# A two-layer graph kernel on one core: first-layer products two slots behind instead of three, the per-turn chain and the held-back products at other slots

## The chip, the cores and the metric

One core of one Trainium2 chip runs the whole kernel. The time is the device time of one execution in microseconds (us). The engines are TensorE (PE, matmuls; PEld is its weight load), VectorE (DVE), ScalarE (ACT), GpSimd (POOL) and SyncE (SP, which here only issues transfers). Sixteen DMA engines move data between memory and the on-chip buffers.

## The reference, cut to what matters

```python
def _L0_gnn_ref(z, dist, W, B):                    # N = 4096, D = 128
    msg = z @ W + B
    sens = exp(-(1.0 / dist - 1.0) ** 2 / 0.5)
    return where(dist < 1.0, sens, 0.0) @ msg      # 4096x4096 @ 4096x128

def _L1_gnn_ref(x, adj, W):
    A_hat = adj + eye(4096)
    d = sum(A_hat, axis=1) ** -0.5
    return relu((d[:, None] * A_hat * d[None, :]) @ (x @ W.T))

h = maximum(layernorm(x), 0);  x = x + _L0_gnn_ref(h, adj, L0_W, L0_B)
h = maximum(layernorm(x), 0);  x = x + _L1_gnn_ref(h, adj, L1_W)
```

Both layers multiply by the same 64 MB matrix `adj`, all in float32. The second layer's product for a block of columns needs `support`, the scaled rows of the second layer's input, and those exist only when the first layer has finished the same rows.

## The kernel before, in words

`adj` is cut into 8 by 8 blocks of 512 by 512. The row block is the **turn** g (0 to 7), and the eight column blocks of a turn are visited in the order `ORDER[g]`; each block is a **unit** u = 8g + idx, 0 to 63. Every engine has a hand-written program that loops over the units; what an engine does in its pass u is here called its **slot** u. Engines are tied only by semaphores, so one can be some slots ahead of another, but each keeps its own order.

For unit u: SP loads a pair of units (2 MB in 16 transfers, L282) into one of 3 `raw` buffers. DVE transposes the block into one of 4 `kept` buffers (L651) and writes the masked copy into one of 5 `wt` buffers (`cut`, L666). ACT does the logarithm (L531), the inversion (L536), a square (L541) and the final exponential (L547 or L550), in the order log(u), square(u-1), invert(u), weigh(u-1); in turns 0 to 2 the square of an odd unit is done by DVE instead (`quad`, L672). PE then multiplies: `multiply_weights` (L380) for the unit LAG = 3 slots back, eight matmul instructions into the accumulator `acc0`. A `wt` buffer is free again for `cut(u)` when the products of unit u-5 are done.

The second layer uses the same transposed block. If its column block lies below the turn, `mix_once` (L393) multiplies it at once from `kept`. Otherwise SP writes it to memory (`store`, L293, 1 MB) and it comes back through POOL's queue (L348) for a **late job** `mix_late` (L402), at the slots of the table `JOBS`, the rest in `TAIL`. DVE's transposition of unit u+4 waits until the 1 MB write of unit u has landed. In turns 0 to 2 PE also sums the block's rows (`sum_tiles`, L410); later DVE does that (L659).

Between turns there is a **chain** for the finished row block g-1, spread over slots of turn g: ACT copies the row sums (`copy_sums`, L558, idx 1) and PE turns them (`turn_sums`, L417, idx 2); ACT copies the accumulator (`copy_x1t`, L576, idx 2, after the last product of turn g-1, and before weigh(u-1) on ACT); PE transposes it (L433, idx 3); DVE reads the sums (`own_rows`, L734 or L739, idx 3) and makes the new rows and their normalisation (`make_x1`, L748 to L766, idx 4); ACT takes `log_pows` (L580) and copies (`copy_hid`, L588, idx 4) what PE transposed (`turn_hid`, L439, idx 5); PE multiplies (L445, idx 6); DVE writes `support` (L777, idx 7). In turns 6 and 7 ACT also empties a second-layer bank (`evict`, L592, in its slots 48 and 56), and PE's `mix_once` of those slots waits for it.

The masks for the row sums (`make_quads`, L723 and L726, 20 small DVE instructions) are made in DVE's slot 2. At the head DVE has only `take_moments(0)` (from L687) before the first `adj` pair lands.

The order within PE's slot before the change, which the change rearranges:

```python
if 1 <= g <= PE_SUMS and idx == 2: turn_sums(g - 1)
if g < PE_SUMS: sum_tiles(u)
if at_once(u) and idx < G - 1 and not (g >= 6 and idx == 0): mix_once(u)
if g >= 1 and idx == 3: turn_x1(g - 1)
if g >= 1 and idx == 5: turn_hid(g - 1)
if u >= LAG: multiply_weights(u - LAG)
if g >= 1 and idx == 6: multiply_support(g - 1)
# then the late jobs of u, then mix_once of the last idx
```

Of the kernel before, what the change touches and what calls it, by code (L numbers as in the profile page):

```python
# [18 lines left out]
G = 8  # L19
# [2 lines left out]
B = 32  # L22
T = 4
RAW, KEPT, WTS, LATE = 3, 4, 5, 3
LAG = 3
PAIRS = G * C4
UNITS = 2 * PAIRS

# [27 lines left out]
def once_count(u):  # L56
# [2 lines left out]

JOBS = {17: [(0, 0)], 25: [(0, 1)], 28: [(1, 1)],
# [4 lines left out]
TAIL = [(2, 6), (3, 6), (4, 6), (5, 6), (6, 6), (0, 5), (0, 6), (1, 6),  # L67
        (2, 7), (3, 7), (4, 7), (5, 7), (6, 7), (7, 7), (0, 7), (1, 7)]
IN_TURN = [job for u in sorted(JOBS) for job in JOBS[u]]
# [5 lines left out]
PE_SUMS = 3  # L75


def squared_by_dve(u):

    return u < PE_SUMS * G and u % 2 == 1  # L80


def dve_squares(u):
# [25 lines left out]
def slot_count(j):  # L109

    return sum(late_slot(i) == late_slot(j) for i in range(j + 1))


def build(nc, x, adj, w0, b0, w1, out):
# [6 lines left out]
    with ctx:  # L121
# [230 lines left out]
        def _(pe):  # L352
# [44 lines left out]
            def mix_late(j, bank, start, stop):  # L397
                r, c = LOADED[j]
                slot = late_slot(j)
                pe.wait_ge(late_loaded[slot], 16 * slot_count(j))  # L400
                for k in range(T):
                    mm = nc.tensor.matmul(bank[:], support[:, c * T + k, :], late_tile(slot)[:, k, :],  # L402
                                          start=(start and k == 0), stop=(stop and k == T - 1))
                mm.then_inc(late_done, 1)
# [9 lines left out]
            def turn_sums(g):  # L414
                pe.wait_ge(sums_copied, g + 1)
                for a in range(T):
                    mm = nc.tensor.matmul(side[:, a:a + 1], hid_t[:, a * P:(a + 1) * P], thirty_second[:],  # L417
                                          start=True, stop=True)
                mm.then_inc(quads_summed, 1)

            def sum_quads(g):
                pe.wait_ge(summed, C4 * (g + 1 - PE_SUMS))
                if g == PE_SUMS:
                    pe.wait_ge(quads_done, 2)
                nc.tensor.matmul(side[:, 0:T * Q * C4], quad_sum[:].rearrange("p q i -> p (q i)"),
                                 rowpart[:, g % 2].rearrange("p a q c -> p (a q c)"),
                                 start=True, stop=True).then_inc(quads_summed, 1)
# [8 lines left out]
            def turn_hid(g):  # L436
                pe.wait_ge(hid_done, g + 1)
                for a in range(T):
                    last = nc.tensor.transpose(side[:, a * P:(a + 1) * P], hid[:, a, :], ident[:])  # L439
                last.then_inc(hid_turned, 1)  # L440

            def multiply_support(g):
                pe.wait_ge(hid_t_done, g + 1)
                for a in range(T):
                    mm = nc.tensor.matmul(side[:, a * P:(a + 1) * P], hid_t[:, a * P:(a + 1) * P], w1t[:],  # L445
                                          start=True, stop=True)
                mm.then_inc(sup_multiplied, 1)
# [8 lines left out]
            for u in range(UNITS):  # L456
                g, idx = u // G, u % G
                if g == 0 and idx % 2 == 0:
                    turn_h0(idx // 2)
                    multiply_msg(idx // 2)  # L460
                if 1 <= g <= PE_SUMS and idx == 2:
                    turn_sums(g - 1)
                if g > PE_SUMS and idx == 1:
                    sum_quads(g - 1)
                if g < PE_SUMS:
                    sum_tiles(u)
                if at_once(u) and idx < G - 1 and not (g >= 6 and idx == 0):
                    mix_once(u)
                if g >= 1 and idx == 3:
                    turn_x1(g - 1)  # L470
                if g >= 1 and idx == 5:
                    turn_hid(g - 1)
                if u >= LAG:
                    multiply_weights(u - LAG)
                if g >= 1 and idx == 6:
                    multiply_support(g - 1)
                for i, (r, c) in enumerate(JOBS.get(u, [])):
                    mix_late(first_job(u) + i, mix[r], r == 0 and c == 0, (r, c) in ((0, 4), (1, 5)))
                if g >= 6 and idx == 0:
                    mix_once(u)  # L480
                if g >= 1 and idx == G - 1:
                    mix_once(u)
# [14 lines left out]
            for t, (r, c) in enumerate(TAIL):  # L497
                if t == 0:
                    sum_quads(G - 1)
                if t < LAG:  # L500
                    multiply_weights(UNITS - LAG + t)
                if t == 4:
                    turn_x1(G - 1)
                if t == 5:
                    turn_hid(G - 1)
                if t == 6:
                    multiply_support(G - 1)
                if (r, c) == (1, 6):
                    pe.wait_ge(sup_done, G)
                if c == G - 1 and r == 2:  # L510
                    pe.wait_ge(sup_done, G)
                if (r, c) == (G - 1, G - 1):
                    for k in range(T):
                        mm = nc.tensor.matmul(tail_bank[r][:], support[:, c * T + k, :],
                                              kept[:, (UNITS - 2) % KEPT, k, :], start=False, stop=(k == T - 1))
                    mm.then_inc(late_done, 1)
                else:
                    mix_late(loads, tail_bank[r], (r, c) in ((0, 5), (1, 6)), c == G - 1)
                    loads += 1
                if c == G - 1:  # L520
                    ended += 1
                    if ended >= 2:
                        turn_out(ended - 2)
# [3 lines left out]
        def _(act):  # L527
# [50 lines left out]
            def log_pows(g):  # L578
                act.wait_ge(pows_done, g + 1)
                nc.scalar.activation(inv[:], pows[:], ACT.Ln).then_inc(pows_ln, 1)  # L580
# [5 lines left out]
            def copy_hid(g):  # L586
                act.wait_ge(hid_turned, g + 1)
                nc.scalar.copy(hid_t[:], side[:]).then_inc(hid_t_done, 1)  # L588
# [11 lines left out]
            for u in range(UNITS):  # L600
                g, idx = u // G, u % G
                log(u)
                if u >= 1 and not squared_by_dve(u - 1):
                    square(u - 1)
                if g >= 1 and idx == 4:
                    log_pows(g - 1)
                invert(u)
                if g >= 1 and idx == 2:
                    copy_x1t(g - 1)
                if u >= 1:  # L610
                    weigh(u - 1)
                if g == 0 and idx in (1, 3, 5):
                    std_rows((idx + 1) // 2)
                    copy_h0((idx + 1) // 2)
                if 1 <= g <= PE_SUMS and idx == 1:
                    copy_sums(g - 1)
                if g >= 6 and idx == 0:
                    evict(g - 6)
                if g >= 1 and idx == 4:
                    exp_pows(g - 1)  # L620
                    copy_hid(g - 1)
            square(UNITS - 1)
            weigh(UNITS - 1)
            copy_x1t(G - 1)
# [13 lines left out]
        def _(dve):  # L638
# [140 lines left out]
                last.then_inc(sup_done, 1)  # L779

            take_moments(0)
            for u in range(UNITS):
                g, idx = u // G, u % G
                turn(u)
                if g < PE_SUMS:
                    cut(u)
                    if u >= 1 and squared_by_dve(u - 1):
                        quad(u - 1)
                elif u >= 1 and squared_by_dve(u - 1):
                    quad(u - 1)  # L790
                if idx % 2 == 1 and g >= PE_SUMS:
                    row_sum(u // 2)
                if g == 0 and idx % 2 == 0:
                    invert_std(idx // 2)
                    if idx < 6:
                        take_moments(idx // 2 + 1)
                    if idx == 2:
                        make_quads()
                elif g == 0:
                    make_msg(idx // 2)  # L800
                if g >= 1 and idx == 3:
                    own_rows(g - 1)
                if g >= PE_SUMS:
                    cut(u)
                if g >= 1 and idx == 4:
                    make_x1(g - 1)
                if g >= 1 and idx == 7:
                    make_support(g - 1)
            own_rows(G - 1)
            make_x1(G - 1)  # L810
# [54 lines left out]
```

## Time and profile before

| | |
|---|---|
| median of 3 runs | 616.36 us (614.26, 616.36, 616.45) |
| profiled execution | 612.92 us, of which span 611.1 us |
| mean granted TensorE clock | 0.958 of full |
| PE busy | 530.7 us, 87% |
| DVE busy | 484.6 us, 79% |
| ACT busy | 465.2 us, 76% |
| moved by DMA | 145.19 MB, 238 GB/s on average |

The span runs from the first to the last instruction; the execution has 1.8 us more around it. "Busy" is the sum over an engine's instructions; a "granted clock" of 1.00 is 2.4 GHz and of 0.5 is 1.2 GHz. The DMA share is the mean busy share of the 16 DMA engines, and can come out a little above 1.

### The profile page before, as it was taken

To read this page: it belongs to the slowest core of one execution; us is meant where nothing else is said; L and a number is where in the kernel's file an instruction comes from. 1 tells how busy PE (TensorE), PEld (TensorE's weight loads), DVE (VectorE), ACT (ScalarE), POOL (GpSimd) and SP (SyncE) were. 2 spreads that over 40 slices of the span, in tenths; PEclk is the share of its full clock that TensorE was granted. 3 is DMA by queue.
4 is the path that set the end of the run, shared out by engine and by line. 5 is a ranking of instruction groups with operands and counts; after the bars stand their busy time and mean duration, and the time that the engine had idled before them with its cause. 6 is when DMAs were issued, how large, how long until landed. Compare 5 with 4: busy or idle time off the path is not lost.

```text
span 611.1 us, 4804 instructions
## 1 busy us (share of the span) xinstructions
PE 530.7 (87%) x1509; PEld 241.9 (40%) x1509; DVE 484.6 (79%) x555; ACT 465.2 (76%) x306; POOL 39.6 (6%) x68
## 2 busy tenths in 40 slices
PE   2446897789869999688999999799999999999994
PEld 1233443233324444333444444344444444445442
DVE  2899998689978899999999989965999589102156
ACT  2387898799889879999999899984999497910010
POOL 0340500000000000000000000000000000201000
PEclk9997997979998999899899999989999999999998
DMA  7999999999999589979997799896798410497122
GB/s 172 222 257 313 322 303 323 325 312 285 338 319 308 130 241 312 309 175 316 320 234 206 207 297 309 240 224 188 232 238 242 113 52 21 163 423 305 69 66 73
DMA packets 93340, 145.19 MB, mean 238 GB/s; under 512 B 10369, under 2 KB 84354, under 8 KB 84354
## 3 DMA queue, kind: packets, MB, share of 16 engines
q1 hardware_dynamic: 88274, 108.17, 65.9%
q0 software_dynamic: 5040, 36.70, 16.3%
q8 instruction: 12, 0.20, 0.1%
q14 instruction: 14, 0.11, 0.1%
HBM read 106.04 MB, written 38.80 MB: 237 GB/s over the span
## 4 chain that ended last, share of the span: by engine, by line
PE 50%; ACT 25%; DVE 18%; issue 4%; SPq 2%; DMA 1%; DVEq 0%
PE acc L380 18%; PE mix L393 12%; PE mix L402 12%; ACT wt L531 6%; ACT wt L541 6%; DVE kept L651 6%; ACT wt L550 5%; ACT wt L536 5%; DVE wt L666 4%; DVE wt L672 2%; PE acc L402 2%; PE mix L410 1%; DVE msg L713 1%; PE side L402 1%; SPq L282 1%
## 5 line engine op out<-in xcount | busy, mean ns | idle before, releaser
L380 PE MATMUL acc<-wt,msg 128*128 128x512 f32 x512 | 239.5, 612 | 4.7 <-ACT wt L550 4.7
L666 DVE SCALAR_TENSOR_TENSOR wt<-kept 128x2048 f32<-128x2048 f32 x64 | 146.5, 2289 | 21.1 <-PE acc L380 19.7
L651 DVE STREAM_TRANSPOSE kept<-raw 128x2048 f32<-128x2048 f32 x64 | 147.5, 2304 | 7.3 <-DMA raw<-in_adj_dram 5.7
L380 PEld LDWEIGHTS acc<-wt,msg 128*128 128x128 f32 x512 | 97.5, 197 | 130.4 <-issue 123.9
L531 ACT ACTIVATE wt<-wt 128x2048 f32<-128x2048 f32 x64 | 121.9, 1905 | 25.4 <-DVE wt L666 25.4
L536 ACT ACTIVATE wt<-wt 128x2048 f32<-128x2048 f32 x64 | 121.7, 1901 | 0.3
L393 PE MATMUL mix<-kept,support 128*128 128x512 f32 x224 | 103.7, 609 | 7.8 <-ACT mixed L592 4.7
L550 ACT ACTIVATE wt<-wt 128x2048 f32<-128x2048 f32 x52 | 98.8, 1901 | 0.0
L541 ACT ACTIVATE wt<-wt 128x2048 f32<-128x2048 f32 x52 | 98.8, 1900 | 0.0
L402 PE MATMUL mix<-late,support 128*128 128x512 f32 x208 | 93.5, 592 | 0.0
L659 DVE TENSOR_REDUCE rowpart<-raw 128x16 f32<-128x4096 f32 x20 | 87.6, 4378 | 0.0
L393 PEld LDWEIGHTS mix<-kept,support 128*128 128x128 f32 x224 | 42.9, 195 | 62.8 <-issue 54.3
L402 PEld LDWEIGHTS mix<-late,support 128*128 128x128 f32 x208 | 39.3, 190 | 48.3 <-issue 48.3
L410 PE MATMUL mix<-kept,ones 128*32 128x512 f32 x192 | 31.1, 726 | 23.9 <-DVE kept L651 23.9
L348 POOL DMA_DIRECT2D late<-adj_t_spill x26 | 13.9, 535 | 468.4 <-PE mix L402 391.5
L672 DVE SCALAR_TENSOR_TENSOR wt<-wt 128x2048 f32<-128x2048 f32 x12 | 27.5, 2289 | 17.3 <-ACT wt L536 17.3
L576 ACT COPY x1t<-acc 128x512 f32<-128x512 f32 x8 | 4.6, 580 | 41.5 <-PE acc L380 41.5
L748 DVE TENSOR_TENSOR x<-side,x 128x512 f32<-128x512 f32 x8 | 5.5, 688 | 28.6 <-PE side L433 28.6
L635 ACT COPY kept<-mix 128x512 f32<-128x512 f32 x6 | 3.5, 585 | 29.9 <-PE mix L402 26.6
L333 POOL TENSOR_SCALAR support<-x,mv 128x128 f32<-128x128 f32 x24 | 20.1, 856 | 47.1 <-DVE mv L691 47.1
L547 ACT ACTIVATE wt<-wt 128x2048 f32<-128x2048 f32 x12 | 22.8, 1898 | 0.0
L819 DVE TENSOR_TENSOR kept<-mix,support 128x512 f32<-128x512 f32 x6 | 4.1, 690 | 19.2 <-PE mix L491 19.2
(87 smaller groups left out, 256.7 us busy)
## 6 DMA issues: line engine op xcount, KB each, us to landing
raw<-in_adj_dram SPq DMA_DIRECT2D x512, 128.0 KB, 5.7
adj_t_spill<-kept SPq DMA_DIRECT2D x35, 1024.0 KB, 10.2
late<-adj_t_spill POOLq DMA_DIRECT2D x26, 1024.0 KB, 7.9
raw<-adj_t_spill POOLq DMA_DIRECT2D x9, 1024.0 KB, 9.1
x<-in_x_dram SPq DMA_DIRECT2D x32, 64.0 KB, 2.8
out_dram<-kept SPq DMA_DIRECT2D x32, 64.0 KB, 1.8
w_sb<-in_L_gnn_W_dram SPq DMA_DIRECT2D x1, 64.0 KB
late<-in_L_gnn_W_dram SPq DMA_DIRECT2D x1, 64.0 KB
```

The source lines that it names most:

```text
L380: mm = nc.tensor.matmul(acc0[:], msg[:, col(u) * T + k, :], wt[:, u % WTS, k, :], start=(first and k == 0), stop=(last and k == T - 1))
L393: mm = nc.tensor.matmul(once_bank[g][:], support[:, c * T + k, :], kept[:, u % KEPT, k, :], start=(first and k == 0), stop=False)
L402: mm = nc.tensor.matmul(bank[:], support[:, c * T + k, :], late_tile(slot)[:, k, :], start=(start and k == 0), stop=(stop and k == T - 1))
L410: mm = nc.tensor.matmul(bank[k * B:(k + 1) * B, :], ones[:], kept[:, u % KEPT, k, :], start=(u % G == 0), stop=(u % G == G - 1))
L531: nc.scalar.activation(v, v, ACT.Ln, bias=LN_GUARD).then_inc(ln_done, 1)
L536: nc.scalar.activation(v, v, ACT.Exp, scale=-1.0).then_inc(inv_done, 1)
L541: nc.scalar.activation(v, v, ACT.Square, bias=-1.0).then_inc(square_done, 1)
L550: nc.scalar.activation(v, v, ACT.Exp, scale=-2.0).then_inc(wt_done, 1)
L651: nc.vector.transpose(dst, src).then_inc(turned, 1)
L659: nc.vector.tensor_reduce(dst, src, AX_X, ALU.add).then_inc(summed, 1)
L666: nc.vector.scalar_tensor_tensor(out=wt[:, u % WTS], in0=v, scalar=CUTOFF, in1=v, op0=ALU.is_lt, op1=ALU.mult).then_inc(cut_done, 1)
L672: nc.vector.scalar_tensor_tensor(out=v, in0=v, scalar=-2.0, in1=v, op0=ALU.add, op1=ALU.mult).then_inc(quad_done, 1)
```

## The change

`LAG` goes from 3 to 2, so PE's products in slot u are those of unit u-2. The late jobs move to other slots, 20 in all as before: turn 1 gets one (before none), turn 2 two more instead of one, turn 3 two, turn 4 three, turn 5 four, and turns 6 and 7 four each instead of five. In turns 1 to 4 the chain's steps come one slot earlier (on DVE the last one two slots), in turns 5 to 7 they stay at their slots, while PE's steps `turn_hid` and `multiply_support` now stand at the head of their slot. `copy_sums` and `turn_sums` come one slot earlier. In turn 0 DVE squares two units (3 and 7) instead of four, ACT the other six. `make_quads` moves ahead of the first unit. `mix_late` waits for its own part of `support`.

```diff
-LAG = 3
+LAG = 2
-JOBS = {17: [(0, 0)], 25: [(0, 1)], 28: [(1, 1)],
-        33: [(0, 2)], 35: [(1, 2)], 38: [(2, 2)],
-        41: [(0, 3)], 43: [(1, 3)], 45: [(2, 3)], 47: [(3, 3)],
-        48: [(0, 4)], 49: [(1, 4)], 51: [(2, 4)], 53: [(3, 4)], 55: [(4, 4)],
-        56: [(1, 5)], 57: [(2, 5)], 59: [(3, 5)], 61: [(4, 5)], 63: [(5, 5)]}
+JOBS = {15: [(0, 0)], 22: [(0, 1)], 23: [(1, 1)],
+        30: [(0, 2)], 31: [(1, 2)], 33: [(2, 2)],
+        38: [(0, 3)], 39: [(1, 3)], 41: [(2, 3)], 43: [(3, 3)],
+        46: [(0, 4)], 47: [(1, 4)], 49: [(2, 4)], 51: [(3, 4)], 53: [(4, 4)],
+        55: [(1, 5)], 57: [(2, 5)], 59: [(3, 5)], 61: [(4, 5)], 63: [(5, 5)]}
 def squared_by_dve(u):
-    return u < PE_SUMS * G and u % 2 == 1
+    return u < PE_SUMS * G and u % (4 if u < G else 2) == (3 if u < G else 1)
+EARLY_TURNS = 5
+STEPS = {"own_rows": (2, 3), "copy_x1t": (1, 2), "turn_x1": (2, 3), "make_x1": (3, 4), "copy_hid": (3, 4),
+         "turn_hid": (4, 5), "multiply_support": (5, 6), "make_support": (5, 7), "sum_quads": (1, 1)}
+def step_at(g, idx, name):
+    return g >= 1 and idx == STEPS[name][g >= EARLY_TURNS]
@@ mix_late
+                pe.wait_ge(sup_done, c + 1)
@@ PE, slot u
-                if 1 <= g <= PE_SUMS and idx == 2:
-                    turn_sums(g - 1)
-                if g > PE_SUMS and idx == 1:
+                if g > PE_SUMS and step_at(g, idx, "sum_quads"):
                     sum_quads(g - 1)
+                if step_at(g, idx, "turn_hid"):
+                    turn_hid(g - 1)
+                if step_at(g, idx, "multiply_support"):
+                    multiply_support(g - 1)
                 if g < PE_SUMS:
                     sum_tiles(u)
                 if at_once(u) and idx < G - 1 and not (g >= 6 and idx == 0):
                     mix_once(u)
-                if g >= 1 and idx == 3:
+                if 1 <= g <= PE_SUMS and step_at(g, idx, "sum_quads"):
+                    turn_sums(g - 1)
+                if step_at(g, idx, "turn_x1"):
                     turn_x1(g - 1)
-                if g >= 1 and idx == 5:
-                    turn_hid(g - 1)
                 if u >= LAG:
                     multiply_weights(u - LAG)
-                if g >= 1 and idx == 6:
-                    multiply_support(g - 1)
@@ PE, tail
-                if t == 4:
+                if t == 3:
                     turn_x1(G - 1)
-                if c == G - 1 and r == 2:
-                    pe.wait_ge(sup_done, G)
@@ ACT, slot u
-                if g >= 1 and idx == 4:
-                    log_pows(g - 1)
                 invert(u)
-                if g >= 1 and idx == 2:
+                if step_at(g, idx, "copy_x1t"):
                     copy_x1t(g - 1)
                 if u >= 1:
                     weigh(u - 1)
-                if 1 <= g <= PE_SUMS and idx == 1:
+                if 1 <= g <= PE_SUMS and idx == 0:
                     copy_sums(g - 1)
-                if g >= 1 and idx == 4:
+                if step_at(g, idx, "copy_hid"):
+                    log_pows(g - 1)
+                    copy_hid(g - 1)
                     exp_pows(g - 1)
-                    copy_hid(g - 1)
@@ DVE
             take_moments(0)
+            make_quads()
-                    if idx == 2:
-                        make_quads()
-                if g >= 1 and idx == 3:
-                    own_rows(g - 1)
                 if g >= PE_SUMS:
                     cut(u)
-                if g >= 1 and idx == 4:
+                if step_at(g, idx, "own_rows"):
+                    own_rows(g - 1)
+                if step_at(g, idx, "make_x1"):
                     make_x1(g - 1)
-                if g >= 1 and idx == 7:
+                if step_at(g, idx, "make_support"):
                     make_support(g - 1)
```

## Rows read from the trace of the kernel before

**Rows 1.** The page, its first part: busy time of each engine.

```profile
PE 530.7 (87%) x1509; PEld 241.9 (40%) x1509; DVE 484.6 (79%) x555; ACT 465.2 (76%) x306; POOL 39.6 (6%) x68
```

**Rows 2.** Busy time by stretches: us, PE, PEld, DVE, ACT, POOL busy, clock, DMA share, GB/s.

```profile
31.00:93.00 62.00, 45.84 (x184) 23.61 (x184) 61.38 (x109) 53.31 (x40) 15.00 (x20) 0.89 1.04 303
93.00:145.00 52.00, 41.62 (x138) 17.23 (x135) 41.79 (x43) 44.26 (x30) 0.00 (x0) 0.87 1.08 318
215.00:293.00 78.00, 66.28 (x168) 29.90 (x167) 77.48 (x56) 75.38 (x47) 1.58 (x3) 0.96 0.98 275
397.00:400.00 3.00, 2.58 (x3) 1.17 (x4) 3.00 (x2) 3.00 (x3) 0.00 (x0) 0.50 1.02 282
400.00:603.00 203.00, 202.02 (x528) 93.38 (x526) 117.68 (x150) 117.23 (x80) 11.03 (x21) 0.99 0.55 174
```

**Rows 3.** Waits over the whole span: us in total, times, longest.

```profile
ACT x1t L576 <- PE acc L380: 41.5, 6, 13.0
```

**Rows 4.** DVE in order of time: start, us, then the instruction, idle before.

```profile
40.97 1.25 DVE L723 TENSOR_REDUCE quad_sum<-ident 128x32 f32<-128x128 f32 x4
42.12 3.19 DVE L726 TENSOR_REDUCE own_quad<-ident 128x4 f32<-128x128 f32 x16
...
93.79 2.31 DVE L651 STREAM_TRANSPOSE kept<-raw 128x2048 f32<-128x2048 f32 x1 [0.46 <-DMA adj_t_spill<-kept]
...
106.95 2.31 DVE L651 STREAM_TRANSPOSE kept<-raw 128x2048 f32<-128x2048 f32 x1 [1.14 <-DMA adj_t_spill<-kept]
...
117.02 2.29 DVE L672 SCALAR_TENSOR_TENSOR wt<-wt 128x2048 f32<-128x2048 f32 x1 [5.43 <-ACT wt L536]
...
122.20 2.31 DVE L651 STREAM_TRANSPOSE kept<-raw 128x2048 f32<-128x2048 f32 x1
```

**Rows 5.** SP's queue in order of time: the block writes of turns 0 and 1.

```profile
82.77 1.29 SPq L293 DMA_DIRECT2D adj_t_spill<-kept  x2
...
96.61 0.95 SPq L293 DMA_DIRECT2D adj_t_spill<-kept  x2
...
109.75 0.90 SPq L293 DMA_DIRECT2D adj_t_spill<-kept  x2
...
122.74 2.13 SPq L293 DMA_DIRECT2D adj_t_spill<-kept  x2
```

**Rows 6.** The block writes L293 issued from 90 to 105 us.

```profile
DMA to landing us min/median/max: 10.2/11.2/12.2
```

**Rows 7.** ACT in order of time: waits, and logarithms of units 16, 24, 38, 39.

```profile
109.20 0.58 ACT L576 COPY x1t<-acc 128x512 f32<-128x512 f32 x1 [4.30 <-PE acc L380]
...
148.01 1.90 ACT L531 ACTIVATE wt<-wt 128x2048 f32<-128x2048 f32 x1
...
208.90 1.91 ACT L531 ACTIVATE wt<-wt 128x2048 f32<-128x2048 f32 x1 [2.76 <-DVE wt L666]
...
314.03 1.91 ACT L531 ACTIVATE wt<-wt 128x2048 f32<-128x2048 f32 x1
...
321.23 1.91 ACT L531 ACTIVATE wt<-wt 128x2048 f32<-128x2048 f32 x1
```

**Rows 8.** PE in order of time: bursts and starts after idle time.

```profile
109.09 1.06 PE L410 MATMUL mix<-kept,ones 128*32 128x512 f32 x8
...
332.94 0.33 PE L425 MATMUL side<-rowpart,quad_sum 128*128 128x64 f32 x2
...
368.38 3.60 PE L402 MATMUL mix<-late,support 128*128 128x512 f32 x8
371.81 3.60 PE L380 MATMUL acc<-wt,msg 128*128 128x512 f32 x8
...
397.42 6.47 PE L393 MATMUL mix<-kept,support 128*128 128x512 f32 x8 [3.95 <-ACT mixed L592]
...
468.45 3.67 PE L393 MATMUL mix<-kept,support 128*128 128x512 f32 x8 [0.77 <-ACT mixed L592]
```

**Rows 9.** A group of instructions by line: count, busy us, mean ns.

```profile
L672 DVE SCALAR_TENSOR_TENSOR wt<-wt 128x2048 f32<-128x2048 f32 x12 | 27.5, 2289 | 17.3 <-ACT wt L536 17.3
```

## The prediction

> **What bounds the kernel now.** I read the page first, then the stretches, the waits, and each engine in order of time. The page says that no engine is idle for long: PE 87%, DVE 79%, ACT 76% [rows 1]. So the average decides nothing, and the stretches must be read. In 31 to 93 us (turn 0) DVE is busy 61.4 of 62 us while ACT has 53.3 and PE 45.8, and the DMA engines are full as well, share 1.04 [rows 2]. In 93 to 145 us, about turn 1, no compute engine is full (41 to 44 of 52 us), yet the DMA share is 1.08. From 215 to 293 us DVE and ACT are full, PE is not. From 400 us to the last product near 602 us PE is full, 202.0 of 203 us, and ACT has 117 [rows 2].
>
> Turn 1 loses time in one knot. ACT stands 4.30 us before it copies the accumulator at 109.20 [rows 7], DVE then stands 5.43 us for ACT's inversion and squares at 117.02, and the unit transposed next after the one at 106.95 comes only at 122.20 [rows 4]. Each waits for work that stands behind the other's in a fixed order. The same shape returns in turn 2. ACT's wait for PE at this copy is 41.5 us in six times [rows 3], but the longest ones fall where PE is full anyway and cost nothing.
>
> The prices: ACT's logarithms of units 38 and 39 are 7.20 us apart with four activations between them, so one activation is 1.80 [rows 7]. A group of eight PE instructions starts 3.43 us after the one before it in a full stretch [rows 8]; I call it one product, 3.43. Row sums on PE are 1.0 (the 1.06 at 109.09, less the overlap) [rows 8].
>
> **The head and turn 0.** Twenty small instructions leave DVE's slot 2: from 40.97 to 45.31, 4.3 us [rows 4]. They now fall before the first block lands at 17.2 us, after DVE's moments end at 11.5, and 11.5 + 4.3 = 15.8, so they cost nothing there. Two squares leave DVE (2.29 each [rows 9]) and two of 1.80 come to ACT, which has 8.7 us idle in 31 to 93 us [rows 2]. DVE would reach unit 8 some 6 to 9 us earlier. I count **0** for all this, because of what is late next: the transposition at 93.79 (unit 10) waited for the write of unit 6, and that at 106.95 (unit 12) for the write of unit 8 [rows 4]. SP issued that last write at 96.61 [rows 5], and writes of that time land 10.2 us or more later [rows 6], so at 106.8. SP is not late for DVE: its writes go out at 82.77, 96.61, 109.75 and 122.74, 13.1 us apart [rows 5], with 4.19 MB in each step (one 2.10 MB pair, two writes), 320 GB/s at a full DMA share. The bounds are 0 and 8.9 us (4.3 plus two squares); no transfer goes away, so I take 0.
> The Trainium skill, "DMA: Bandwidth & Descriptors", Specifications, gives 358 GB/s of memory bandwidth for a core. By that a step would be 11.7 us instead of 13.1 and turn 0 could give back some 5 us. The trace shows 320 with the engines full, and the sum goes by that.
>
> **Turn 1.** The chain steps come a slot earlier. With products two behind, the last product of turn 0 is in PE's slot 9, ACT's copy is in its slot 9 after three other activations, and neither waits. Count ACT from unit 10: transposed from 93.7, masked 4.6 us later, logarithm at 98.3. Slots 10 to 15 have three activations each and three squares, 21 x 1.80 = 37.8, small copies 0.8, and 2.8 of waiting for masks where DVE has a square or `make_x1` ahead. Logarithm of unit 16: 98.3 + 37.8 + 0.8 + 2.8 = 139.7, before 148.01 [rows 7]: **-8.3**. The writes allow it: that of unit 12 goes out at 122.74 and lands at 133, the transposition of unit 16 needs it at 132.4.
>
> **Turn 2.** 28 activations, 50.4, and copies 1.7. The copy of slot 17 waits about 1.9 for PE, which has the new late job and the at-once product of slot 15 in front of it; the wait of 2.76 at unit 24 [rows 7] stays, as there the mask stands behind a square. 139.7 + 50.4 + 1.7 + 1.9 + 2.8 = 196.5, before 208.90: **-12.4** so far. The writes need unit 24 not before 187, the transposition is then at 189.
>
> **Turns 3 and 4: given back.** What the new table puts late is PE, just before each copy of the accumulator. From the moment unit 20's weights are ready PE has, in slots 22 to 25, nine products and 2 us of sums, 32.9; ACT reaches its copy after 29.5 (slots of 5.4, 7.2, 2.8, 5.9, 2.8, 5.4). **+3.4**. In slots 30 to 33 it is nine products and 0.3, 31.2, against 3 x 7.20 + 5.4 = 27.0: +4.2. Slots 26 to 29 are light, so PE stands there over 3 us between products. After such an idle time of 3.95 us at 397.42 a group took 6.47 instead of 3.43 [rows 8], at a granted clock of 0.50, the lower level of 1.2 GHz [rows 2]: 3.0 more, **+7.2** together. Neither wait is in the trace; the lower bound of both is 0 (PE ahead by its at-once products), the upper 10.6, and I take the upper since ACT is full there and cannot catch up. Net at unit 38's logarithm: 314.03 - 12.4 + 3.4 + 7.2 = 311.2 to 312.2; I take 312.2, with 1 us for DVE, which has nearly no idle time either [rows 2] and now waits for PE's step at slot 29.
>
> **Turn 5 to the end: PE.** Slot 38's first product can go when unit 36's weights are ready, at 312.2. Two products to 319.1; slot 39's three from 319.4 to 329.7; slot 40's two to 336.6. Before, slot 40 ended at 332.94 (where slot 41 begins) [rows 8]. **+3.7**. From there on PE is full in both. Late jobs in slots 41 to 63 are 12 instead of 14, and one product of weights less is outstanding: 3 x 3.43 = **-10.3**. The evictions of slots 48 and 56 find their jobs done in slots 46 and 55, so PE's waits of 3.95 and 0.77 and the 3.0 at the low clock [rows 8] go: **-7.8**. Against that, the job of slot 46 needs `support` of block 4, which DVE makes in its slot 47: behind it on PE stand all later products. DVE made it 2 us before PE will want it by this count; bounds 0 and 5, I take **+1**. In turns 5 to 7 the copy (slot idx 2) stands before the first product of the turn on the same slot; ACT is then over a slot ahead, 0. The late jobs' loads on POOL's queue go with the jobs, and a slot ring of three gives each more than 10 us, 0. The tail's `turn_x1` one step earlier has its copy ready, 0.
>
> **Sum.** +3.7 - 10.3 - 7.8 + 1.0 = -13.4 on the profiled execution of 612.9 (span 611.1 and 1.8 around it), 599.5. The median of the runs was 616.4, 3.4 above the profiled one; the runs of the changed kernel should lie as high: **603**. By the sum the gain of turns 1 and 2 mostly dies in turns 3 and 4, and what counts is what PE no longer has to do after slot 40.
>
> **The rivals.**
> *No crowding before the copies.* PE does more of its at-once products before the weights come and ACT never stands: the 10.6 of turns 3 and 4 stay won, 592. For it: PE had 11.7 us idle in 215 to 293 us. Against: that idle time lies in light slots.
> *The transfers set turns 1 and 2.* Share 1.08 in turn 1 [rows 2]; two more late blocks of 1.05 MB are fetched by the end of turn 2, and any transfer that comes later delays the write behind it, then unit u+4. The 8.3 of turn 1 are lost: 611. Against it: before, SP was ahead of DVE by unit 16.
> Beside that, the same page of the Trainium skill, section "Issuing engines are not separate DMA queues", says that POOL's and SP's transfers share the 16 engines, so a second queue hides none of these fetches.
> *The stall only moves.* The chain is shifted by a slot and so are its inputs; PE's `turn_hid` at slot 12 waits for DVE, ACT's copy behind weigh(10) for PE, and unit 13 is as late as before. Then +12.4: 615, no change.
> *Slower: products two behind catch PE cold.* In slots without at-once or late products PE now has to wait for ACT's last activation of the slot before, and falls to 1.2 GHz. Each such start that lies on the path costs 3.0 [rows 8]. One is in my sum; more than five in all turn the gain to a loss, eight give 603 + 7 x 3.0 = 624. Against it: where PE decides, from slot 40, it always has work in front.
>
> **How the numbers follow.** Chances: the sum 0.44, no crowding 0.20, transfers 0.16, stall moved 0.11, cold PE 0.09. Half a per cent (3 us) is about what a measurement of this kernel can tell from no change, so faster means below 613.3: 0.44 + 0.20 + 0.16 = 0.80; same 0.11; slower 0.09. The range from 592 to 614 takes in both bounds of the crowding and the transfers' case, and leaves out the last two, 0.20.
>
> **What would show it.** In the changed profile: DVE idle 5 us or more before units 10 and 12, waiting for writes, at nearly the old times (93.8, 107); no idle time over 2 us around unit 13; logarithm of unit 16 near 140, of 24 near 197; ACT waiting for PE at the copies of slots 25 and 33; slot 41's quad sum on PE near 337; no wait for L592 near 390. A logarithm of unit 24 above 205 makes turns 1 and 2 wrong; one of unit 38 below 305 the crowding; gaps on PE after 400 us the last part.

## The result, and the profile after

| | before | changed |
|---|---|---|
| median of 19 runs | 616.01 us (613.1 to 616.6) | 612.81 us (609.6 to 615.5) |
| profiled execution | 612.92 us | 611.06 us |

The ratio is 0.9960, interval 0.9946 to 0.9974: faster beyond the interval, but by 0.4 per cent where 2.2 were forecast. The time lies inside the stated range of 592 to 614 us; the gain is about a fifth of the forecast one. The profiled execution was to be 599.5 us and took 611.06.

The first part of the page of the changed kernel shows nothing of it, except that PE is busy 6.4 us less and ACT 3.8 more than in [rows 1]:

```profile
PE 524.3 (86%) x1509; PEld 237.8 (39%) x1509; DVE 480.5 (79%) x553; ACT 469.0 (77%) x308; POOL 41.4 (7%) x68
```

The busy time by stretches of the changed kernel, columns as in [rows 2]:

```profile
31.00:93.00 62.00, 50.24 (x205) 25.20 (x206) 53.31 (x87) 60.00 (x45) 16.76 (x20) 0.88 1.05 308
...
93.00:145.00 52.00, 42.63 (x144) 16.55 (x143) 49.98 (x45) 49.49 (x32) 0.00 (x0) 0.97 1.08 314
215.00:293.00 78.00, 63.73 (x154) 27.97 (x153) 73.78 (x67) 72.14 (x45) 1.58 (x3) 0.96 0.97 283
340.00:400.00 60.00, 53.03 (x133) 24.08 (x132) 48.14 (x44) 52.85 (x35) 2.11 (x4) 0.97 0.76 224
400.00:600.00 200.00, 197.44 (x518) 91.08 (x517) 121.04 (x150) 119.90 (x81) 10.50 (x20) 1.00 0.57 176
```

In turn 1 ACT now works 49.5 of 52 us where it had 44.3: the knot is gone. In turn 0 the two full engines have changed places: ACT is busy 60.0 of 62 us, DVE 53.3. And between 340 and 400 us, where the forecast had PE full, PE, ACT and DVE each have about 7 us of idle time or more. ACT in order of time, the same instructions as in [rows 7] and the copies that wait:

```profile
95.50 0.57 ACT L587 COPY x1t<-acc 128x512 f32<-128x512 f32 x1
...
139.44 1.89 ACT L542 ACTIVATE wt<-wt 128x2048 f32<-128x2048 f32 x1
...
197.46 1.91 ACT L542 ACTIVATE wt<-wt 128x2048 f32<-128x2048 f32 x1 [2.76 <-DVE wt L676]
...
216.05 0.59 ACT L587 COPY x1t<-acc 128x512 f32<-128x512 f32 x1 [4.36 <-PE acc L392]
...
279.74 0.59 ACT L587 COPY x1t<-acc 128x512 f32<-128x512 f32 x1 [4.81 <-PE acc L392]
...
311.51 1.90 ACT L542 ACTIVATE wt<-wt 128x2048 f32<-128x2048 f32 x1
...
369.36 0.59 ACT L599 COPY hid_t<-side 128x512 f32<-128x512 f32 x1 [6.77 <-PE side L452]
...
370.43 1.91 ACT L542 ACTIVATE wt<-wt 128x2048 f32<-128x2048 f32 x1 [0.38 <-DVE wt L676]
...
375.85 1.89 ACT L561 ACTIVATE wt<-wt 128x2048 f32<-128x2048 f32 x1
```

The copy of slot 9 waits for nothing. The logarithm of unit 16 is at 139.44 (forecast 139.7), that of unit 24 at 197.46 (196.5), and the crowding before the copies of slots 25 and 33 is there, 4.36 and 4.81. Unit 38 comes at 311.51 (312.2). PE in order of time shows slot 41 beginning at 337.16 (336.6), and what follows:

```profile
337.16 0.33 PE L438 MATMUL side<-rowpart,quad_sum 128*128 128x64 f32 x2
...
357.98 0.60 PE L446 MATMUL side<-ident,x1t 128*128 128x128 f32 x4
...
368.72 0.60 PE L452 MATMUL side<-ident,hid 128*128 128x128 f32 x4
369.16 3.60 PE L392 MATMUL acc<-wt,msg 128*128 128x512 f32 x8
372.59 1.05 PE L458 MATMUL side<-w1t,hid_t 128*128 128x128 f32 x8
377.80 5.11 PE L392 MATMUL acc<-wt,msg 128*128 128x512 f32 x8 [4.15 <-ACT wt L561]
385.72 3.67 PE L415 MATMUL mix<-late,support 128*128 128x512 f32 x8 [2.82 <-DVE support L787]
...
454.24 3.70 PE L392 MATMUL acc<-wt,msg 128*128 128x512 f32 x8 [1.05 <-ACT wt L561]
...
469.20 3.67 PE L405 MATMUL mix<-kept,support 128*128 128x512 f32 x8 [0.96 <-ACT mixed L603]
...
523.48 3.70 PE L392 MATMUL acc<-wt,msg 128*128 128x512 f32 x8 [0.55 <-ACT wt L561]
```

PE does stand, in slot 46: 4.15 us for unit 44's weights, the product then partly at the low clock (5.11 us for 3.43; the granted clock is 0.50 from 377.8 to 379.5), 2.82 us for `support`. Two engines make the weights late. One is DVE, in order of time:

```profile
342.51 2.30 DVE L661 STREAM_TRANSPOSE kept<-raw 128x2048 f32<-128x2048 f32 x1
344.85 2.29 DVE L676 SCALAR_TENSOR_TENSOR wt<-kept 128x2048 f32<-128x2048 f32 x1
358.62 0.69 DVE L758 TENSOR_TENSOR x<-side,x 128x512 f32<-128x512 f32 x1 [11.48 <-PE side L446]
...
361.60 2.30 DVE L661 STREAM_TRANSPOSE kept<-raw 128x2048 f32<-128x2048 f32 x1
363.82 4.38 DVE L669 TENSOR_REDUCE rowpart<-raw 128x16 f32<-128x4096 f32 x1
368.12 2.28 DVE L676 SCALAR_TENSOR_TENSOR wt<-kept 128x2048 f32<-128x2048 f32 x1
```

DVE has the masks of unit 44 ready at 347 and stands 11.5 us at `make_x1`, until PE's slot 43 has transposed the new rows. Only then it makes the masks of unit 45 (8.8 us for transposition, row sum and mask). ACT's logarithm of unit 45 follows at 370.43, and unit 44's weights, three activations behind that, at 377.7.

The other is ACT itself, in the lines shown above. In its slot 44 it stands 6.77 us at `copy_hid`, until PE's `turn_hid`, at the head of PE's slot 45, has come at 368.72. PE has no idle time before `turn_hid`. Only behind this copy comes the logarithm of unit 45, and it then waits just 0.38 us more for DVE's masks. So the two waits run side by side and end almost together. From `turn_hid` to unit 44's weights ACT needs 9.0 us, while PE has one product and `multiply_support`, 4.9 us; the difference is PE's wait. **The idle time of DVE and ACT looks harmless there, since PE is the full engine; but the work queued behind it is late.**

### The profile page after: what moved, and what is told of

The parts are those of the page before. It is cut to its first block, busy times and chain, and to the rows that moved or that the text cites. A ratio compares the mean times of both kernels' runs of the same rounds, so it can differ in the third digit from the quotient of the medians.

```text
span 609.3 us, 4840 instructions
## 1 busy us (share of the span) xinstructions
PE 524.3 (86%) x1509; PEld 237.8 (39%) x1509; DVE 480.5 (79%) x553; ACT 469.0 (77%) x308; POOL 41.4 (7%) x68
## 4 chain that ended last, share of the span: by engine, by line
PE 45%; ACT 19%; DVE 14%; SPq 11%; DMA 5%; issue 4%; DVEq 0%
PE acc L392 14%; PE mix L405 14%; PE mix L415 12%; SPq L294 10%; DVE kept L661 6%; ACT wt L561 5%; DMA adj_t_spill<-kept 5%; ACT wt L542 4%; ACT wt L552 4%; ACT wt L547 4%; DVE wt L676 3%; PE acc L415 2%; PE side L415 1%; DVE wt L682 1%; DVE rowpart L669 1%
## 5 line engine op out<-in xcount | busy, mean ns | idle before, releaser
L661 DVE STREAM_TRANSPOSE kept<-raw 128x2048 f32<-128x2048 f32 x64 | 147.5, 2304 | 12.3 <-DMA adj_t_spill<-kept 10.3
L542 ACT ACTIVATE wt<-wt 128x2048 f32<-128x2048 f32 x64 | 121.7, 1902 | 21.9 <-DVE wt L676 21.9
L547 ACT ACTIVATE wt<-wt 128x2048 f32<-128x2048 f32 x64 | 121.5, 1899 | 0.3
L561 ACT ACTIVATE wt<-wt 128x2048 f32<-128x2048 f32 x54 | 102.5, 1899 | 0.0
L552 ACT ACTIVATE wt<-wt 128x2048 f32<-128x2048 f32 x54 | 102.5, 1897 | 0.0
L405 PE MATMUL mix<-kept,support 128*128 128x512 f32 x224 | 100.6, 594 | 1.0 <-ACT mixed L603 1.0
L423 PE MATMUL mix<-kept,ones 128*32 128x512 f32 x192 | 27.2, 641 | 10.8 <-DVE kept L661 10.6
L599 ACT COPY hid_t<-side 128x512 f32<-128x512 f32 x8 | 4.6, 575 | 28.1 <-PE side L452 28.1
L682 DVE SCALAR_TENSOR_TENSOR wt<-wt 128x2048 f32<-128x2048 f32 x10 | 22.9, 2287 | 3.3 <-ACT wt L547 3.3
L345 POOL TENSOR_SCALAR support<-x,mv 128x128 f32<-128x128 f32 x24 | 21.9, 930 | 40.1 <-DVE mv L701 40.1
```

Of the source, the lines that this page charges most:

```text
L405: mm = nc.tensor.matmul(once_bank[g][:], support[:, c * T + k, :], kept[:, u % KEPT, k, :], start=(first and k == 0), stop=False)
L542: nc.scalar.activation(v, v, ACT.Ln, bias=LN_GUARD).then_inc(ln_done, 1)
L547: nc.scalar.activation(v, v, ACT.Exp, scale=-1.0).then_inc(inv_done, 1)
L552: nc.scalar.activation(v, v, ACT.Square, bias=-1.0).then_inc(square_done, 1)
L561: nc.scalar.activation(v, v, ACT.Exp, scale=-2.0).then_inc(wt_done, 1)
L661: nc.vector.transpose(dst, src).then_inc(turned, 1)
```

## The experiments

Theory: the gain was lost in turn 5 by these waits, beside the crowding in turns 3 and 4. Rivals: PE's products after slot 40 cost more in another way; two behind costs PE in every slot; the table of late jobs is what brings the gain. Ratios are to the kernel before, timed beside each kernel, as (ratio, interval).

**The changed kernel again.**

> The changed kernel unaltered, as the yardstick on the same chip as the three runs beside it: 0.996 of the kernel before, in its profile a wait of DVE of about 11.5 us for PE's transposition of the new rows in slot 44, of ACT of about 6.8 at copy_hid in slot 44, and of PE of about 4.2 and 2.8 in slot 46.

612.4 us (0.9963, 0.9942 to 0.9985). The waits return: 11.81 at `make_x1` in slot 44, PE's longest wait for weights 4.2. The pattern is no accident of one execution.

**Free DVE and ACT in turns 5 to 7.** The name `copy_hid` in the table stands for all of ACT's group: `log_pows`, the copy and `exp_pows`.

```diff
-STEPS = {... "make_x1": (3, 4), "copy_hid": (3, 4), ...}
+STEPS = {... "make_x1": (3, 5), "copy_hid": (3, 5), ...}
```

> Turns 5 to 7 only: make_x1 on DVE and log_pows, copy_hid, exp_pows on ACT one slot later (idx 5). Theory: the gain is lost in turn 5 because DVE stands 11.5 us at make_x1 in slot 44 with the masks of unit 45 behind it, so with products two behind PE finds no weights in slot 46 and no support; with DVE free to make these masks first PE stays full: its waits of 4.15 and 2.82 and 1.7 us at the low clock go, and the 2.6 of turns 6 and 7, so 7 to 11 us less than the changed kernel, ratio to before 0.980 to 0.985. Rival (PE's products after slot 40 simply cost more in another way, by the clock or by the late blocks' loads): no difference over 2 us from the changed kernel.

600.6 us (0.976, 0.973 to 0.979), 12 us less than the changed kernel timed beside it, a little more than expected. DVE of this kernel in order of time:

```profile
359.66 2.28 DVE L676 SCALAR_TENSOR_TENSOR wt<-kept 128x2048 f32<-128x2048 f32 x1
361.86 0.68 DVE L758 TENSOR_TENSOR x<-side,x 128x512 f32<-128x512 f32 x1
```

its ACT:

```profile
370.89 1.91 ACT L561 ACTIVATE wt<-wt 128x2048 f32<-128x2048 f32 x1
...
372.79 0.57 ACT L599 COPY hid_t<-side 128x512 f32<-128x512 f32 x1
```

and its PE:

```profile
360.06 0.60 PE L446 MATMUL side<-ident,x1t 128*128 128x128 f32 x4
...
375.56 3.60 PE L392 MATMUL acc<-wt,msg 128*128 128x512 f32 x8
380.24 3.67 PE L415 MATMUL mix<-late,support 128*128 128x512 f32 x8 [1.08 <-DVE support L787]
```

The masks of unit 45 are now made (359.66) before the new rows, which come when PE's transposition at 360.06 is done anyway, without a wait. ACT's last activation for unit 44 (370.89) now stands before the copy, which waits for nothing. Unit 44's product at 375.56 follows PE's work before it without idle time. The place of two groups of instructions, with no work added or taken, is worth more than the whole change.

Both groups were moved at once, and no run moved one alone. By the rows of the changed kernel neither would have done much alone in turn 5 (an estimate): with only DVE free, ACT's copy still ends at 369.84 and just the 0.38 us go; with only ACT's copy moved, unit 45's masks still come at 370.4. In turn 6 the pair returns (7.42 us at the copy, then 0.39 for the masks); in turn 7 only ACT's copy stands, 9.89 us. So what is shown is the worth of both moves together.

**The old table in the changed kernel** (`JOBS` of before, all else changed).

> The changed kernel with the table of late jobs of before. Theory: ACT's waits of 4.4 and 4.8 us at the copies of slots 25 and 33 go, the logarithm of unit 38 comes 9 us earlier than in the changed kernel, slot 41 starts on PE 10 to 14 us earlier, but 2 more late jobs stand after it and the evictions cost PE some 4 us again: 604 to 611, ratio 0.983 to 0.993. Rival (the new table is what brings the gain there is, by taking work from the full stretch): slower than the changed kernel, ratio 1.000 or more.

604.7 us (0.9834, 0.9809 to 0.986). The copies of slots 25 and 33 wait 0 and 0.86 us, unit 38 is at 303.56 (8.0 us earlier, where 9 were expected), slot 41 begins at 325.78, 11.4 earlier. So the new table alone costs the changed kernel 8 us; the rival that it brings the gain falls.

**Two behind alone** (`LAG = 2` in the kernel before).

> The kernel before with products two slots behind and nothing else changed. Theory: the wait of 4.3 at the copy of slot 10 goes and the knots of turns 1 and 2 get shorter, 5 to 9 us less at unit 24, but turn 5 gives part of it back in PE waits, since two behind leaves PE no spare product when DVE stands at make_x1: 608 to 614, ratio 0.987 to 0.998, with PE waits of over 3 us in slots 44 to 48. Rival (two behind costs PE in every slot, the other parts pay for it): slower than before, ratio over 1.003.

615.3 us (1.0002, 0.9985 to 1.0019): a miss of both. Unit 24 comes 6.8 us earlier (202.07), as expected, but slot 41 only 1.8 (331.13). The waits of this kernel, in us in total, times, longest, have one that the kernel before has not:

```profile
PE acc L380 <- ACT x1t L576: 11.3, 4, 4.9
```

With three behind, the first product of a turn stands a slot after ACT's copy of the accumulator; with two it is in the same slot, and PE waits for ACT: 0.8, 2.2, 4.9 and 3.4 us in turns 1 to 4. The changed kernel, with the copy a slot earlier in these turns, has no such wait. What these waits cost is not shown, and the early chain was not run with three behind.

What turn 5 was expected to give back is there, but smaller: PE waits 1.61 and 2.61 us for weights in slots 46 and 47, where over 3 was expected, and 8.9 us in five times from slot 41 to the end, where the kernel before has no such wait. ACT's `copy_hid` of slot 44 waits 2.77 us and the masks behind it 0.49. So the loss in turns 5 to 7 comes with two behind, also without the other parts of the change.

**The old head in the changed kernel.** Masks for the row sums in slot 2, units 1, 3, 5, 7 squared by DVE.

> The changed kernel with turn 0 as before: the masks made in DVE's slot 2 and units 1, 3, 5, 7 squared by DVE. Theory: the writes of units 6 and 8 set when units 10 and 12 can be transposed, so the head's 8.9 us of DVE work are worth nothing there: within 0.3 per cent of the changed kernel (610 to 614), logarithm of unit 12 within 2 us of 112.6. Rival (the savings of the head carry on to turn 1): 3 us or more slower than the changed kernel, 615 or more.

614.0 us (0.9992, 0.997 to 1.0014): 0.3 per cent above the changed kernel, inside the bound, but the logarithm of unit 12 is at 116.06, 3.4 later than 112.64 (and the changed kernel's second profile had it at 111.38), where under 2 was expected.

**Half the writes.**

```diff
-sp.dma_start(spill[u // G, col(u)], kept[:, u % KEPT]...)
+sp.dma_start(spill[u // G, col(u)][:, 0:2 * ROWS], kept[:, u % KEPT, 0:2]...)
-pool.dma_start(late_tile(slot)..., spill[r, c])
+for h in range(2):
+    pool.dma_start(late_tile(slot)[:, 2 * h:2 * h + 2]..., spill[r, c][:, 0:2 * ROWS])
```

> The changed kernel writing only the first half of each transposed block to memory and reading that half twice, so the second half of the late blocks' product is of other data: 512 KB instead of 1 MB to write, the reads as before. Theory (the writes set units 8, 10 and 12): DVE's waits for them (10.3 us in five times) go, logarithm of unit 12 three to seven us earlier than 112.6, but ACT's copies in turns 3 and 4 and the stand in turn 5 stay: 606 to 611. Rival (these units wait for something else that lands at the same time, or the raw loads bind): logarithm of unit 12 within 1.5 us of the changed kernel's.

609.65 us (0.9908, 0.9882 to 0.9934). All of DVE's waits for the writes are gone, but unit 12's logarithm is at 112.20, as in the changed kernel (112.64): the theory's number for it is missed and the reason with it, though the time was in its range. The rival's number is met, but neither of its reasons: DVE waits for raw loads 1.7 us in all, as in the changed kernel. What holds turn 0 there is seen in the same stretch of this kernel:

```profile
31.00:93.00 62.00, 49.28 (x204) 24.39 (x205) 57.22 (x89) 59.98 (x45) 17.79 (x22) 0.97 1.05 277
```

ACT, with the two squares that it got from DVE, is busy 60.0 of 62 us, as in the changed kernel, and from 76.8 us to unit 12's logarithm it waits once, 0.97 us. So the writes held DVE, but ACT set the pace. The run is 3 us faster than the changed kernel by its ratio; its profiled execution is only 0.9 us shorter in span (608.4 for 609.3), so where these 3 us come from is left open.

**The transposition later** (in turns 5 to 7 PE's `turn_x1` behind `multiply_weights`).

> The changed kernel with PE's transposition of the new rows in turns 5 to 7 one product (3.4 us) later in its slot, behind multiply_weights. Nothing else. It makes the suspected cause larger. Theory (DVE's stand at make_x1 is what makes unit 45's weights and the support late): DVE's wait in slot 44 grows from 11.5 to about 15 us, PE's waits in slot 46 by 3.4 in all, and in turns 6 and 7 by up to 3 each: 616 to 621. Rival (it has slack): no more than 1 us slower.

618.9 us (1.0074, 1.0045 to 1.0103). The dose works: PE's wait in slot 46 grows from 4.15 by 3.44,

```profile
380.62 5.83 PE L392 MATMUL acc<-wt,msg 128*128 128x512 f32 x8 [7.59 <-ACT wt L563]
```

exactly one product; that for `support` is 2.10. Its ACT shows through which of the two waits it came:

```profile
368.74 0.59 ACT L601 COPY hid_t<-side 128x512 f32<-128x512 f32 x1 [3.99 <-PE side L452]
...
373.25 1.91 ACT L544 ACTIVATE wt<-wt 128x2048 f32<-128x2048 f32 x1 [3.82 <-DVE wt L678]
```

The copy ends no later than in the changed kernel, and the wait for DVE's masks behind it grows from 0.38 to 3.82 us, by the same 3.44. So DVE's side is the later one, by 0.38 us in the changed kernel, and all that is added to it reaches PE. DVE's own wait was 10.9 and not 15: it came to `make_x1` 3.4 us later too (350.5 for 347.1). What counts is when the wait ends (361.4 for 358.6, in an execution whose slot 41 began 0.6 us earlier), not how long it is.

**Free order and old table.**

> Both changes that helped in one: make_x1 and copy_hid of turns 5 to 7 one slot later, and the table of late jobs of before. Theory (two separate losses, the crowding before the copies in turns 3 and 4 and DVE's stand in turn 5): PE waits of 0.71 and 3.50 and 2.9 us at the low clock in turn 5 go from the run with the old table, and 1 to 2 of turns 6 and 7: 595 to 599, ratio 0.967 to 0.974. Rival (each helps only because the other loss is there, PE full otherwise): 600 or more, as one of them alone.

597.1 us (0.9701, 0.9673 to 0.9728). The two losses are separate, though not quite additive: by the ratios 12 and 8 us alone, 16 together, so about 4 us are common to both.

**Free order, late jobs in light slots.**

```diff
+JOBS = {18: [(0, 0)], 26: [(0, 1)], 28: [(1, 1)], 30: [(0, 2)], 34: [(1, 2)], 36: [(2, 2)],
+        38: [(0, 3)], 41: [(1, 3)], 44: [(2, 3)], 45: [(3, 3)],
+        47: [(0, 4)], 48: [(1, 4)], 49: [(2, 4)], 51: [(3, 4)], 53: [(4, 4)],
+        55: [(1, 5)], 57: [(2, 5)], 59: [(3, 5)], 61: [(4, 5)], 63: [(5, 5)]}
```

> The same free order with the 20 late jobs in slots where PE has no at-once product, away from the copies of slots 17, 25, 33: 18, 26, 28, 30, 34, 36, 38, 41, 44, 45, 47, 48, then as in the changed kernel. Theory: ACT does not wait over 1 us at those copies, 4 us less than with the old table because one or two late jobs fewer stand in the full stretch: 591 to 596, ratio 0.960 to 0.969. Rival: the gaps on PE in light slots cost nothing, so filling them brings nothing, and it is as the run with the old table.

593.5 us (0.9641, 0.9613 to 0.967). The copy of slot 33 waits 2.18 us, not under 1; the rest is as expected. From 372 us on PE has no idle time up to the last `adj` product.

**The same with the old head.**

> The run with late jobs in light slots, with turn 0 as before (masks for the row sums in slot 2, DVE squaring units 1, 3, 5, 7). Theory: the head is worth little, as the writes set units 10 and 12; the run of the changed kernel with the old head was 0.3 per cent slower, so 0 to 4 us slower than 593.5 here: ratio 0.963 to 0.971. Rival (its 8.9 us of DVE work come out where nothing later hides them): 6 us or more slower, 600 or more.

594.7 us (0.968, 0.9653 to 0.9707): the head is worth 0.4 per cent here, though the two intervals overlap.

**The masks of units 24 and 25 first.** In that kernel DVE writes them ahead of the square of unit 23 and of the row sum.

```diff
+elif u in (PE_SUMS * G, PE_SUMS * G + 1):
+    cut(u)
+    if squared_by_dve(u - 1): quad(u - 1)
...
-if g >= PE_SUMS: cut(u)
+if g >= PE_SUMS and u > PE_SUMS * G + 1: cut(u)
```

> The run with late jobs in light slots, and DVE writing the masks of units 24 and 25 ahead of its square of unit 23 and its row sum. Theory: ACT's waits of 2.76 and 2.60 us for these masks go, ACT is full up to slot 38 so the 5 us are carried to PE's full stretch: 3 to 5 us less than that run, 588 to 591, ratio 0.955 to 0.960. Rival (PE or the transfers of turn 3 set it): no change, 593.

590.45 us (0.9596, 0.957 to 0.9621), 4 per cent under the kernel before and the best found. ACT's logarithms of units 24 and 25, in order of time:

```profile
193.43 1.89 ACT L542 ACTIVATE wt<-wt 128x2048 f32<-128x2048 f32 x1
...
199.44 1.91 ACT L542 ACTIVATE wt<-wt 128x2048 f32<-128x2048 f32 x1
```

Neither waits (2.76 and 2.60 in the run with light slots), and slot 41 begins 2.9 us earlier (323.35 for 326.21). Not all of the 5.4 us arrives: the copy of slot 25 now waits 3.29 us for PE, where it waited for nothing.

**The free order in the kernel before.**

> The kernel before with only make_x1, log_pows, exp_pows and copy_hid of turns 5 to 7 one slot later. Theory: DVE stands only 1.5 us at make_x1 in slot 44 there and products three behind have weights in stock, so it brings nothing: ratio 0.997 to 1.003. Rival (the order of turns 5 to 7 was a loss before as well, and its mending has nothing to do with the change): ratio under 0.99.

615.9 us (1.0005, 0.9986 to 1.0024): nothing. DVE in the kernel before, in order of time:

```profile
350.60 2.29 DVE L666 SCALAR_TENSOR_TENSOR wt<-kept 128x2048 f32<-128x2048 f32 x1 [0.65 <-PE acc L380]
...
354.40 0.69 DVE L748 TENSOR_TENSOR x<-side,x 128x512 f32<-128x512 f32 x1 [1.51 <-PE side L433]
```

With three behind DVE stands 1.5 us there and not 11.5, ACT's copy of slot 44 waits for nothing, and PE has a product more in stock. The 10 us between the two stands are 5.8 by which DVE comes earlier in the changed kernel (347.1 for 352.9) and 4.2 by which PE's transposition comes later (357.98 for 353.76). Full `wt` buffers held DVE by only 0.65 us of that. The loss by this order is a cost of the change, not an old one.

## Why the prediction was wrong, point by point

PE's time in the profiled executions splits at the start of slot 41, which is where the forecast split it:

| | slot 41 begins | to the start of the last product group | late jobs from slot 41 |
|---|---|---|---|
| before | 332.94 | 265.8 | 14 |
| changed | 337.16 | 259.7 | 12 |
| forecast for the changed | 336.6 | 248.7 (265.8 - 17.1) | 12 |
| changed, free order | 339.23 | 248.8 | 12 |
| old table | 325.78 | 265.9 | 14 |
| old table, free order | 326.73 | 257.2 | 14 |
| light slots, free order | 326.21 | 253.7 | 13 |

**Turns 1 to 4: right.** -8.3 was -8.6, -12.4 was -11.4, +3.4 was +4.4, and +7.2 was +4.8: the low clock that I had added in slots 30 to 33 did not show (the products there took 3.6 to 3.7). The forecast of slot 41 was off by 0.6, and that close only by luck: two terms missed by 1.0 each in one direction and one by 2.4 in the other. The run with the old table confirms the crowding by taking it away.

**Turn 5 to the end: the step that failed.** "From there on PE is full in both", and with it "ACT is then over a slot ahead, 0". The terms -10.3 and -7.8 were right as far as work goes: the run with the free order takes 248.8, the forecast 248.7. Between the two lie 11 us: 4.15 for the weights, 1.7 at low clock, 2.82 for `support` of which 1 was in the sum, 1.05, 0.96 and 0.55 in turns 6 and 7, 10.2 in all; the other 0.7 is not accounted for. I carried PE's count through turn 5 and looked at ACT only at the copy of slot 42. I never followed DVE, whose `make_x1` stands ahead of the masks of unit 45 and waits for PE, nor ACT at `copy_hid`, which stands ahead of the last activation for unit 44 and waits for PE as well. The count could have been made from the trace of the kernel before: from PE's transposition, 3.0 of `make_x1`, 8.7 to unit 45's mask, 7.2 of ACT, 19 us, while PE has four products and small work there, 15.7. On ACT's side it is 9 us from `turn_hid` on, against one product and `multiply_support`. Three behind, PE has a product more in either count.

**The support wait** was given bounds 0 and 5 and taken as 1; it measured 2.82. DVE's slot 47 came late; with both groups moved the wait is 1.08, as forecast.

**Turn 0: 0, and the wrong reason.** Unit 8's logarithm came 3.7 us earlier (83.78 for 87.43) and unit 12's 6, and the run with the old head shows 3.4 of it at unit 12 to be the head's and about 0.3 per cent at the end. The writes were given as what is late next; DVE did wait for them (10.3 us in five times), but without these waits unit 12 comes no earlier, since ACT was full.

The Trainium skill's 358 GB/s ("DMA: Bandwidth & Descriptors", Specifications) would, by the estimate in the prediction, have given some 5 us back in turn 0. The changed kernel's transfers reach 308 GB/s in 31 to 93 us and 314 in turn 1, at a DMA share of 1.05 and 1.08, so the measured rate stands.

**The rivals.** "Slower: products two behind catch PE cold" named a real thing, PE waiting for weights, but in the wrong place: it was excluded "where PE decides, from slot 40", and there it happened. Its price of 3.0 us for a start at the low clock was an upper one: it was 1.7 in slot 46 and 2.0 for the groups of 5.4 us in slots 27 and 29, but a group of 6.63 us in slot 27 of the second profiled execution cost 3.2. "No crowding" was wrong for the changed kernel and nearly right as a price: 10.6 us were named, and with the old table 8 are won. "The transfers set turns 1 and 2" fell: unit 16 came 8.6 us earlier at a share of 1.08. "The stall only moves" was wrong for turn 1; in turn 5 there is such a stall, which the kernel before did not have.

**The allowance for the median** (3.4 above the profiled execution) was 1.75 for the changed kernel.

## What to carry to other kernels

When a change shortens the stock between two engines, follow each of the others through the next stage too: an engine with idle time still delays all that stands behind its wait in a fixed order. Look for a second engine that waits at the same point; moving one group may then show nothing until the other is moved too. For every wait in such a list, ask what is queued behind it, when that is needed, and put it first if it is ready. Work moved into idle time must go where the engine is idle for long; just before a hand-over of the chain it holds up the full engine.

## What the runs showed that was not expected

A group at PE's low clock costs only where PE is the bound. In slots 27 and 29 of the changed kernel groups of 5.4 us, at a granted clock of 0.68 on average, stand after idle times of 3.5 and 3.3 us, and ACT, which is full there, goes on without a wait until the next copy of the accumulator. The product of 5.11 us in slot 46 costs its 1.7 us, as PE is the bound there. What still stays open is how the head's 0.3 or 0.4 per cent gets to the end, since two kernels show it and in neither is it clear of the interval, and where the 3 us of the run with half the writes come from.
